# Deep attention stage: the weighted sum of the values issued in one run of 128 passes behind the turn of k, in place of two runs of 64 around it

## The chip, the cores and the metric

The kernel runs on one core of a Trainium2 chip. Its time is the device time of one execution in microseconds (us); lower is better. The engines named below are PE (TensorE, matmuls; its weight loads are listed apart as PEld), ACT (ScalarE), DVE (VectorE), POOL (GpSimd) and SP (SyncE, which issues transfers). They run side by side, each through its own instructions in program order, and wait for each other on semaphores.

## What is computed

The reference is a transformer-like chain of twelve sublayers over an activation of 4 sequences x 512 tokens x 128 values, in float32. The change lies in the sublayer that is called "deep" here: six layers of local attention and a gated feed-forward part, and the chain calls it twice. Cut to the attention:

```python
def local_attention(q, k, v):            # 16 heads of 64, windows of 32
    ...
    bk2, bv2 = (look(bk), look(bv))      # each window sees itself and the one before
    sim = jnp.einsum('bhwie,bhwje->bhwij', bq, bk2) * QK_SCALE
    sim = jnp.where(mask, -jnp.finfo(sim.dtype).max, sim)
    attn = jax.nn.softmax(sim, -1)
    out = jnp.einsum('bhwij,bhwje->bhwie', attn, bv2)
    return out.reshape(b, h, n, d)

def attn_layer(x, Wqkv, qs, ksc, Wo):
    q, k, v = jnp.split(x @ Wqkv, 3, -1)
    q = l2norm(q) * qs                   # and k alike, then both are rotated (rope)
    ...
    out = local_attention(q, k, v)
    return out.transpose(0, 2, 1, 3).reshape(b, n, INNER) @ Wo
```

## The kernel before

A call of the deep sublayer (`deep_pe` and its sisters for the other engines) works through 24 units, a unit being one of the six layers for one of the four sequences. Each unit has four tiles of 128 tokens. One loop over steps `s` from 0 to 103 is written out by hand for every engine, and it is software-pipelined: at step `s` the products of q and k are made for tile `s`, the rotated q and k of tile `s - 1` are turned (transposed), the scores and values of tile `s - 2` are made, and the weighted sum of the values of tile `s - 3` is taken. `t = s % 4` is the place of the step in its unit. What belongs to a unit and not to a tile (output projection, layer norm, feed-forward) is put between these by `t`: the variance and its spread at `t == 0`, three gate products and two of the three "a" products at `t == 1`, the last "a" product, the down projection and the first part of the output projection at `t == 2`, the rest of that projection and the mean at `t == 3`.

On PE a step is, in this order: product of q (L1321), half of the scores with the mask (L1276, L1290), values (L1346), the other half of the scores (L1290), something of the unit, **turn of q** (`turn_pe(..., 0)`, L1334, eight passes of 128x128), **product of k** (L1321, four passes of 512 columns), **first run of the weighted sum** (`mix_open_pe`, L1373, 64 passes), something of the unit at `t == 1`, **turn of k** (`turn_pe(..., 1)`, L1334, eight passes), the mean at `t == 3`, **second run of the weighted sum** (`mix_close_pe`, L1373, 64 passes), work of the unit at `t` 1 and 2, and the turn of the probabilities (L1304). A matmul of float32 shows as two passes in the trace, so 32 matmuls are 64 passes.

The turns of q, of k and of the probabilities and the values share one stretch of PSUM, `turns`. ACT copies each out before the next may be written. For the turn of k this stands in `turn_pe`, and the copy is the line below it on ACT (L1507):

```python
pe.wait_ge(de.deep_roped, 2 * i + half + 1)
if half == 1:
    pe.wait_ge(de.deep_turn_kept, 2 * i + 1)
...
nc.scalar.activation(dst, turns.rearrange("p (c t) -> p c t", t=P), ACT.Copy).then_inc(de.deep_turn_kept, 1)
```

ACT takes its work in a written order too. In a step it copies the turned probabilities (L1518), squares the product of q (L1494), takes a square root (L1501), copies the values (L1534), takes the exponential of the scores (L1511), **copies the turned q** (L1507), squares the product of k (L1494), takes the gelus at `t == 1` (L1550), copies the turned k (L1507) and copies the result of the weighted sum (L1525). The exponential waits for DVE, which takes the maximum of the scores (L1589) and subtracts it (L1596) once the second half of the scores is done. POOL scales the rotated q and k (L1753), which the turns wait for, and divides the probabilities (L1759), which their turn waits for.

Of the kernel before, what the change touches and what calls it, by code (L numbers as in the profile page):

```python
# [21 lines left out]
TILES = T // P  # L22
# [6 lines left out]
PAIRS = LHEADS // 2  # L29
# [16 lines left out]
def program(nc, d, out, sublayers):  # L46
    with ExitStack() as ctx:
# [6 lines left out]
        def bank(i):  # L54
            return psum[:, i * 512:(i + 1) * 512]
# [61 lines left out]
        def apart(eng):  # L117

            eng.sem_inc(g.waits_passed, 1)
# [1102 lines left out]
        ALL = UNITS * TILES  # L1222
# [124 lines left out]
                                            xs[unit_ % 2][:, WIN * wi:WIN * wi + 2 * WIN], vw[:, r, :, :], start=True, stop=True)  # L1347
            last.then_inc(de.deep_v_ready, 1)

        def mix_open_pe(pe, c, j):  # L1350
            i, t = c * ALL + j, j % TILES
            pe.wait_ge(de.deep_probs_kept, i + 1)
            pe.wait_ge(de.deep_v_kept, i + 1)
            pe.wait_ge(deep_v_moved[t], 16 * MOVES * (c * UNITS + j // TILES + 1))
            if j + 1 < ALL:
                pe.wait_ge(de.deep_less_max, i + 2)
            apart(pe)
            mix_pe(j, 0)

        def mix_close_pe(pe, c, j):  # L1360
            mix_pe(j, 1).then_inc(de.deep_pv_done, 1)

        def mix_pe(j, part):

            t = j % TILES
            for pair in range(PAIRS // 2 * part, PAIRS // 2 * (part + 1), 2):
                for jj in range(WPT):
                    for odd in range(2):
                        for r in range(2):
                            side = r ^ odd  # L1370
                            half, col = (pair + odd) // 4, (pair + odd) % 4 * P + jj * WIN
                            to = (pair // 2) * P + jj * WIN
                            last = nc.tensor.matmul(bank(odd)[64 * side:64 * side + 64, to:to + WIN],  # L1373
                                                    V[64 * r:64 * r + 64, WPT * t + jj, (pair + odd) * 64:(pair + odd) * 64 + 64],
                                                    probsT[64 * r:64 * r + 64, half, col:col + WIN], start=True, stop=True)
            return last

        WO_FIRST = 3

# [61 lines left out]
        def deep_pe(pe, c):  # L1441
            for s in range(LAST + 1):
                n, t = s // TILES, s % TILES
# [16 lines left out]
                    turn_pe(pe, c, s - 1, 0)  # L1460
                if s < ALL:
                    qk_pe(pe, c, s, 1)
                if 0 <= s - 3 < ALL:
                    mix_open_pe(pe, c, s - 3)
                if t == 1 and ending:
                    gate_pe(pe, c, n - 2, 1)
                if 0 <= s - 1 < ALL:
# [1 line left out]
                if t == 3 and begun:  # L1469
                    mean_pe(pe, c, n - 1)  # L1470
                if 0 <= s - 3 < ALL:
                    mix_close_pe(pe, c, s - 3)
                if t == 1 and ending:
                    gate_pe(pe, c, n - 2, 2)
                    a_pe(pe, c, n - 2, 0)
# [636 lines left out]
```

## Time and profile before

| | us |
|---|---|
| median of three runs | 4470.68 |
| lowest and highest of them | 4459.03, 4475.77 |
| the profiled execution, its own time | 4482.51 |
| its span in the trace | 4480.8 |
| PE busy in the span | 4247.5 (95%) |
| DVE busy | 3201.0 (71%) |
| ACT busy | 2674.7 (60%) |
| POOL busy | 2127.7 (47%) |

The two calls of the deep sublayer take about 1070 to 2680 us and 2840 to 4460 us of the span, 72% of it. The times of rows are microseconds from the start of the span. A busy PE is not PE at its peak: matmuls are pipelined, and the end that a row gives a run lies behind the start of the next one. So the length of a run is read from its start to the start of what follows.

### The profile page before, as it was taken

What the parts mean: (1) busy time and instruction counts of PE and PEld (TensorE: products, weight loads), DVE (VectorE), ACT (ScalarE), POOL (GpSimd) and SP (SyncE); (2) the same over time, 40 slices, a digit from 0 to 9 for tenths busy, and PEclk for the clock granted to TensorE, in tenths of its full rate; (3) what the DMA queues carried; (4) which work ended last, traced back from release to release, by engine and by line L of the source; (5) the groups of instructions that cost most, each with busy time, mean ns of one, the idle gap of its engine ahead of it and who ended that gap; (6) DMA issues with size and microseconds to landing.
All of it is one profiled execution on the core that took longest, in us unless ns stands there. A gap on an engine that the chain in (4) does not pass through costs nothing.

```text
span 4480.8 us, 148099 instructions
## 1 busy us (share of the span) xinstructions
PE 4247.5 (95%) x66444; PEld 2382.4 (53%) x66444; DVE 3201.0 (71%) x4171; ACT 2674.7 (60%) x3161; POOL 2127.7 (47%) x1151
## 2 busy tenths in 40 slices
PE   7998999867999999999999995799999999999998
PEld 4543433334555555555555552455555555555554
DVE  3564666465777777777777766687787787787784
ACT  1451355323776776776776761576776776776774
POOL 0110000013666666666666640666665665666662
PEclk8898899978999999999999997899999999999998
DMA  2000000001111112111111111111211212121111
GB/s 85 1 2 1 1 1 1 1 0 40 33 29 53 39 28 59 33 53 34 33 53 34 33 28 50 24 33 32 56 33 31 56 33 55 32 58 29 33 33 29
DMA packets 78739, 144.92 MB, mean 32 GB/s; under 512 B 18656, under 2 KB 25120, under 8 KB 76576
## 3 DMA queue, kind: packets, MB, share of 16 engines
q1 hardware_dynamic: 78112, 135.45, 11.7%
q8 instruction: 529, 8.67, 0.8%
q14 instruction: 98, 0.80, 0.1%
HBM read 39.97 MB, written 1.05 MB: 9 GB/s over the span
## 4 chain that ended last, share of the span: by engine, by line
PE 80%; POOL 7%; issue 6%; DVE 5%; ACT 2%; DMA 0%; SPq 0%; POOLq 0%; DVEq 0%; ACTq 0%
PE psum L1321 13%; PE psum L1373 7%; PE psum L1346 7%; PE psum L1334 6%; PE psum L1290 5%; PE psum L681 5%; PE psum L1392 5%; PE psum L1304 4%; PE psum L1422 3%; PE psum L713 3%; PE psum L1438 3%; PE psum L1432 3%; PE psum L735 3%; PE psum L1387 3%; POOL arena L1753 3%
## 5 line engine op out<-in xcount | busy, mean ns | idle before, releaser
L1753 POOL TENSOR_TENSOR arena<-arena 128x1024 f32<-128x1024 f32 x384 | 722.3, 1902 | 883.8 <-ACT arena L1501 883.8
L1747 POOL TENSOR_TENSOR arena<-arena 128x1024 f32<-128x1024 f32 x384 | 907.3, 2363 | 246.3 <-DVE arena L1622 246.3
L1618 DVE TENSOR_TENSOR arena<-psum,arena 128x1024 f32<-128x1024 f32 x384 | 467.6, 1218 | 619.5 <-ACT arena L1494 619.0
L1494 ACT ACTIVATE arena<-psum 128x1024 f32<-128x1024 f32 x384 | 392.0, 1021 | 288.9 <-PE psum L1321 288.9
L1373 PEld LDWEIGHTS psum<-arena 64*64 64x64 f32 x24576 | 396.4, 135 | 211.5 <-issue 211.4
L1507 ACT ACTIVATE arena<-psum 128x1024 f32<-128x1024 f32 x384 | 390.5, 1017 | 194.5 <-PE psum L1334 194.5
L1622 DVE TENSOR_TENSOR arena<-psum,arena 128x1024 f32<-128x1024 f32 x384 | 466.2, 1214 | 0.0
L1629 DVE TENSOR_REDUCE h_pair<-arena 128x16 f32<-128x1024 f32 x384 | 464.1, 1209 | 0.0
L1373 PE MATMUL psum<-arena 64*64 64x32 f32 x24576 | 438.8, 221 | 4.9 <-DVE arena L1596 4.7
L1334 PE MATMUL psum<-w_ident,arena 128*128 128x128 f32 x3072 | 416.4, 279 | 23.0 <-POOL arena L1753 14.7
L1334 PEld LDWEIGHTS psum<-w_ident,arena 128*128 128x128 f32 x3072 | 338.8, 141 | 161.0 <-POOL arena L1753 91.5
L1321 PE MATMUL psum<-deep_wqkv,arena 128*128 128x512 f32 x768 | 382.5, 622 | 26.5 <-DVE arena L1622 19.1
L1759 POOL TENSOR_TENSOR arena<-arena 128x1024 f32<-128x1024 f32 x192 | 365.3, 1902 | 69.8 <-DVE arena L1606 61.0
L1290 PEld LDWEIGHTS psum<-arena 64*32 64x32 f32 x24576 | 293.6, 105 | 169.6 <-issue 159.5
L1321 PE MATMUL psum<-arena 128*128 128x512 f32 x768 | 361.9, 592 | 0.0
L1518 ACT ACTIVATE arena<-psum 128x1024 f32<-128x1024 f32 x192 | 196.5, 1023 | 259.1 <-PE psum L1304 253.2
L1290 PE MATMUL psum<-arena 64*32 64x64 f32 x24576 | 328.2, 223 | 1.5 <-issue 1.4
L681 PE MATMUL psum<-arena 32*128 32x512 f32 (+3 forms) x1024 | 307.5, 600 | 3.3 <-ACT arena L820 2.3
L1511 ACT ACTIVATE arena<-arena 128x1024 f32<-128x1024 f32 x192 | 202.9, 1057 | 175.5 <-DVE arena L1596 175.5
L713 PE MATMUL psum<-arena 32*128 32x512 f32 (+3 forms) x1024 | 303.6, 583 | 1.8 <-ACT arena L845 1.8
L1589 DVE TENSOR_REDUCE arena<-psum 128x16 f32<-128x1024 f32 x192 | 235.1, 1225 | 63.6 <-PE psum L1290 63.6
L845 ACT ACTIVATE arena<-psum 128x512 f32<-128x512 f32 (+3 forms) x344 | 160.9, 515 | 178.6 <-PE psum L713 177.2
(266 smaller groups left out, 6997.6 us busy)
## 6 DMA issues: line engine op xcount, KB each, us to landing
arena<-arena SPq DMA_DIRECT2D x672, 128.0 KB, 2.4
deep_wqkv<-in_deep_wqkv SPq DMA_DIRECT2D x6, 1536.0 KB, 6.9
arena<-in_deep_wqkv SPq DMA_DIRECT2D x6, 1536.0 KB, 6.7
arena<-arena SPq DMA_DIRECT2D x96, 64.0 KB, 2.0
deep_wo<-in_deep_wo SPq DMA_DIRECT2D x6, 512.0 KB, 7.4
arena<-in_deep_wo SPq DMA_DIRECT2D x6, 512.0 KB, 7.4
deep_w<-in_deep_w SPq DMA_DIRECT2D x6, 341.0 KB, 7.6
arena<-in_deep_w SPq DMA_DIRECT2D x6, 341.0 KB, 7.5
```

The source lines that it names most:

```text
L681: nc.tensor.matmul(bank(v % SCORE_BANKS)[:, 0:keys], da_Q[r32, b * SETS + s, x_ * P:(x_ + 1) * P], keys_of(causal, b, s)[r32, 0:keys], sta ...
L713: nc.tensor.matmul(bank(key_at[m])[:, q0:T], kk[r32, kt * P:(kt + 1) * P], da_Q[r32, b * SETS + s, q0:T], start=True, stop=True).then_inc( ...
L1290: last = nc.tensor.matmul(bank(r)[32 * jj:32 * jj + 32, pair * 64:pair * 64 + 64], qT[j % 2][r64, pair, jj * WIN:(jj + 1) * WIN], kT[r64, ...
L1321: last = nc.tensor.matmul(bank(2 + cc), xs[unit_ % 2][:, WIN + t * P:WIN + (t + 1) * P], wqkv[:, half * INNER + cc * 512:half * INNER + (c ...
L1334: last = nc.tensor.matmul(turns[:, m * P:(m + 1) * P], roped[a % 2][:, h:h + 2, :], w.ident[:, :], start=True, stop=True, is_transpose=True)
L1373: last = nc.tensor.matmul(bank(odd)[64 * side:64 * side + 64, to:to + WIN], V[64 * r:64 * r + 64, WPT * t + jj, (pair + odd) * 64:(pair + ...
L1494: nc.scalar.activation(qk_sq[:, HALVES[half], :], qk_half, ACT.Square).then_inc(de.deep_qk_squared, 1)
L1618: nc.vector.tensor_tensor(turned[:, hs, :].rearrange("p h (a e) -> p h a e", a=2), swapped, sin, ALU.mult).then_inc(de.deep_rope_parts, 1)
L1622: nc.vector.tensor_tensor(roped[a % 2][:, hs, :], qk_half, under(tabs[:, 2 * half, t, :], shape), ALU.mult).then_inc(de.deep_rope_parts, 1)
L1629: nc.vector.tensor_reduce(h_pair[:, hs, 0], qk_sq[:, hs, :], AX.X, ALU.add).then_inc(de.deep_sq_summed, 1)
L1747: nc.gpsimd.tensor_tensor(roped[a % 2][:, hs, :], roped[a % 2][:, hs, :], turned[:, hs, :], ALU.add).then_inc(de.deep_summed, 1)
L1753: nc.gpsimd.tensor_tensor(roped[a % 2][:, hs, :], roped[a % 2][:, hs, :], over(h_inv[a % 2][:, hs], [P, LHEADS, LD]), ALU.mult).then_inc(d ...
```

## The change

The two runs of 32 matmuls become one of 64, with the same operands and targets, and it stands where the second run stood. The waits of the first run (for the turned probabilities, the values, their moves and the less-maximum of the next tile) stand ahead of the whole run now. Nothing else is moved, and no other engine's instructions change.

```diff
-        def mix_open_pe(pe, c, j):
+        def mix_pe(pe, c, j):
             i, t = c * ALL + j, j % TILES
             pe.wait_ge(de.deep_probs_kept, i + 1)
             pe.wait_ge(de.deep_v_kept, i + 1)
...
             apart(pe)
-            mix_pe(j, 0)
-
-        def mix_close_pe(pe, c, j):
-            mix_pe(j, 1).then_inc(de.deep_pv_done, 1)
-
-        def mix_pe(j, part):
-
-            t = j % TILES
-            for pair in range(PAIRS // 2 * part, PAIRS // 2 * (part + 1), 2):
+            for pair in range(0, PAIRS, 2):
...
-            return last
+            last.then_inc(de.deep_pv_done, 1)
...
                 if s < ALL:
                     qk_pe(pe, c, s, 1)
-                if 0 <= s - 3 < ALL:
-                    mix_open_pe(pe, c, s - 3)
                 if t == 1 and ending:
                     gate_pe(pe, c, n - 2, 1)
                 if 0 <= s - 1 < ALL:
...
                 if t == 3 and begun:
                     mean_pe(pe, c, n - 1)
                 if 0 <= s - 3 < ALL:
-                    mix_close_pe(pe, c, s - 3)
+                    mix_pe(pe, c, s - 3)
```

On PE, in a step with `t == 2`, the order before was this, from the turn of q to the down projection (a row is a group of equal instructions, with the semaphores that its first one waits for; `arena` holds most tiles):

```order
L1334 MATMUL psum<-w_ident,arena 128x128 [waits deep_v_kept,deep_roped]
L1334 MATMUL psum<-w_ident,arena 128x128 x7
L1321 MATMUL psum<-deep_wqkv,arena 128x512 [waits deep_rope_parts]
L1321 MATMUL psum<-deep_wqkv,arena 128x512
L1373 MATMUL psum<-arena 64x32 [waits deep_less_max,deep_v_moved_3,deep_probs_kept,deep_v_kept]
L1373 MATMUL psum<-arena 64x32 x31
L1334 MATMUL psum<-w_ident,arena 128x128 [waits deep_turn_kept,deep_roped]
L1334 MATMUL psum<-w_ident,arena 128x128 x7
L1373 MATMUL psum<-arena 64x32 x32
L1438 MATMUL psum<-arena,deep_w_0 128x512 [waits deep_hidden_ready]
```

The same place of the changed kernel, where the weighted sum has line 1365 and the down projection line 1430:

```order
L1334 MATMUL psum<-w_ident,arena 128x128 [waits deep_v_kept,deep_roped]
L1334 MATMUL psum<-w_ident,arena 128x128 x7
L1321 MATMUL psum<-deep_wqkv,arena 128x512 [waits deep_rope_parts]
L1321 MATMUL psum<-deep_wqkv,arena 128x512
L1334 MATMUL psum<-w_ident,arena 128x128 [waits deep_turn_kept,deep_roped]
L1334 MATMUL psum<-w_ident,arena 128x128 x7
L1365 MATMUL psum<-arena 64x32 [waits deep_less_max,deep_v_moved_3,deep_probs_kept,deep_v_kept]
L1365 MATMUL psum<-arena 64x32 x63
L1430 MATMUL psum<-arena,deep_w_0 128x512 [waits deep_hidden_ready]
```

The turn of k, which waits for `deep_turn_kept`, now follows the product of k at once; 32 matmuls that stood between them have gone behind it.

## Rows read from the trace of the kernel before

**Rows 1.** Busy time by engine in an early step and in most of a call.

```profile
core 0: us, PE busy (x) PEld busy (x) DVE busy (x) ACT busy (x) POOL busy (x), PEclk, DMA share, GB/s
1120.81:1134.46 13.65, 12.43 (x306) 7.95 (x305) 11.45 (x13) 10.79 (x11) 10.34 (x6) 1.00 0.13 31
1150.00:2640.00 1490.00, 1483.08 (x27972) 876.59 (x27973) 1163.10 (x1325) 1047.87 (x1107) 948.13 (x484) 1.00 0.16 39
```

**Rows 2.** What line 1334, the turns of q and k, waited for: us, times.

```profile
  POOL arena L1753: 106.3, 111
...
  ACT arena L1507: 4.4, 4
```

**Rows 3.** Timeline of PE and ACT, a step with t == 2: start, us.

```profile
2151.91 1.88 PE L1321 MATMUL psum<-deep_wqkv,arena 128*128 128x512 f32 x4
...
2152.49 1.06 ACT L1511 ACTIVATE arena<-arena 128x1024 f32<-128x1024 f32 x1 [0.97 <-DVE arena L1596]
2153.46 1.00 ACT L1507 ACTIVATE arena<-psum 128x1024 f32<-128x1024 f32 x1
...
2153.72 1.14 PE L1373 MATMUL psum<-arena 64*64 64x32 f32 x64
...
2154.79 1.09 PE L1334 MATMUL psum<-w_ident,arena 128*128 128x128 f32 x8
...
2156.88 2.85 PE L1438 MATMUL psum<-arena 128*128 128x512 f32 x6
```

**Rows 4.** Timeline, step 96 of the first call, which has no product of k.

```profile
2658.93 1.00 ACT L1507 ACTIVATE arena<-psum 128x1024 f32<-128x1024 f32 x1
...
2660.08 1.06 PE L1334 MATMUL psum<-w_ident,arena 128*128 128x128 f32 x8 [0.75 <-ACT arena L1507]
...
2661.08 0.78 PE L1373 MATMUL psum<-arena 64*64 64x32 f32 x39
...
2662.05 0.59 PE L1373 MATMUL psum<-arena 64*64 64x32 f32 x25 [0.20 <-issue]
```

**Rows 5.** Timeline of PE, step 98 of the second call, with no turn of k.

```profile
4439.38 2.07 PE L1373 MATMUL psum<-arena 64*64 64x32 f32 x128
4441.37 2.84 PE L1438 MATMUL psum<-arena 128*128 128x512 f32 x6
4444.06 2.74 PE L1387 MATMUL psum<-arena 128*128 128x512 f32 x6
4446.63 4.46 PE L1392 MATMUL psum<-arena 128*128 128x512 f32 x10
```

**Rows 6.** Timeline of PE and ACT, a step with t == 0, and ACT behind it.

```profile
2120.81 1.88 PE L1321 MATMUL psum<-deep_wqkv,arena 128*128 128x512 f32 x4
...
2122.37 1.00 ACT L1507 ACTIVATE arena<-psum 128x1024 f32<-128x1024 f32 x1
...
2126.04 1.09 PE L1304 MATMUL psum<-w_ident,arena 128*128 128x128 f32 x8 [0.19 <-POOL arena L1759]
...
2127.50 1.88 PE L1321 MATMUL psum<-deep_wqkv,arena 128*128 128x512 f32 x4
...
2129.42 1.02 ACT L1494 ACTIVATE arena<-psum 128x1024 f32<-128x1024 f32 x1 [1.23 <-PE psum L1321]
```

**Rows 7.** Timeline of PE and ACT, the step behind it, t == 1.

```profile
2135.01 1.88 PE L1321 MATMUL psum<-deep_wqkv,arena 128*128 128x512 f32 x4
...
2136.58 1.01 ACT L1507 ACTIVATE arena<-psum 128x1024 f32<-128x1024 f32 x1
...
2140.88 1.09 PE L1422 MATMUL psum<-xc,arena 128*85 128x512 f32 x2
```

**Rows 8.** Timeline of PE and ACT, a step with t == 3.

```profile
2105.66 1.04 PE L1334 MATMUL psum<-w_ident,arena 128*128 128x128 f32 x8
...
2106.53 1.89 PE L1321 MATMUL psum<-arena 128*128 128x512 f32 x4
2106.73 1.02 ACT L1507 ACTIVATE arena<-psum 128x1024 f32<-128x1024 f32 x1 [1.79 <-PE psum L1334]
...
2112.36 1.09 PE L1304 MATMUL psum<-w_ident,arena 128*128 128x128 f32 x8
```

## Prediction

> **What bounds the kernel now.** I read the table of busy times by stretch first, to see which engine has no slack in the stage that changes. Over 1490 us of the first call PE is busy for 1483.08, at a granted clock of 1.00, while DVE, ACT and POOL rest for a fifth or more of it [rows 1]. So the stage is as long as PE's passes and waits. A change that only reorders PE can do two things: alter what it costs to go from one kind of pass to another, or let PE run into a wait that other passes had covered.
>
> Next I read the timelines of PE and ACT, one step of each kind, and ask for each wait that the change touches: when does it end, and when does PE get there? The turn of k writes where the turn of q stands, so it waits until ACT has copied q out. In the step with `t == 2` that copy runs from 2153.46 to 2154.46, because it is queued behind the exponential, which itself waited for DVE [rows 3]. PE finishes the product of k and begins the weighted sum at 2153.72. The first run of the sum lasts until 2154.79, so it covers the end of the copy with 0.33 to spare. The list of what line 1334 waited for agrees: ACT's copy held it only 4 times [rows 2]. The change takes this cover away.
>
> **The prices.** All from start to start.
> - After a copy's end the turn of k starts 0.15 later: the copy of [rows 4] ends at 2659.93 and the turn starts at 2660.08. That row is the wait itself, seen in the one step that lacks the product of k.
> - A turn that has waited takes 1.00 to the next run (2660.08 to 2661.08) [rows 4]. An unhindered one takes 0.87 (2105.66 to 2106.53) [rows 8], or 0.109 a pass.
> - A weighted sum in one run of 128 passes takes 1.99, from 4439.38 to 4441.37 [rows 5]. That is the changed kernel's run already. One run of 64 takes 1.07 (2153.72 to 2154.79) [rows 3], two of them 2.14, so joining saves 0.15.
> - A 512-column pass takes 0.43: six take 2.57 (4444.06 to 4446.63) [rows 5]. Four before a sum take 1.81 (2151.91 to 2153.72) [rows 3] where 4 x 0.43 is 1.71, so going over to the small passes costs 0.10.
>
> At this place the Trainium skill has a rule that speaks for the change. Its page TensorEngine Tiling (Key Properties) says that a change of tiling mode drains TensorE. The trace agrees that a switch costs something; by that rule alone the change would gain some 45 us, which is the first rival below, worked out there from rows.
>
> **The change, step by step.** I count from the start of the product of k and ask when the work behind the sum begins.
>
> *t == 2.* The copy ends at 2.55 (2154.46 less 2151.91). Then 0.15, the turn 1.00, the sum 1.99: 5.69. Before it was 4.97 (2156.88 less 2151.91) [rows 3]. Loss **0.72**. PE stands idle from 1.71 to 2.70, some 1.0 us.
>
> *t == 0.* The copy ends at 2.56, so the sum ends at 5.70. Before, the turn of the probabilities began at 5.23, having waited 0.19 for POOL's division [rows 6]; that wait vanishes, and the loss is 0.47. Behind it twelve short passes took 1.46 until 2127.50, more than 12 x 0.109 plus some 0.06 for leaving the small passes, 1.37. I let 0.09 of it be waiting that is now covered. Loss **0.38**.
>
> *t == 1.* Here a gate product of two passes, 0.86, moves in between: PE is there at 1.71 + 0.86 = 2.57. The copy ends at 2.58 (2137.59 less 2135.01), the turn starts at 2.73, the sum ends at 5.72. Before: 5.87 (2140.88 less 2135.01) [rows 7]. Gain **0.15**.
>
> *t == 3.* Much work lies between the scores and the turn of q, so the copy is done at 1.22 (2107.75 less 2106.53) and nothing waits. 1.71 + 0.87 + the mean 0.86 + 0.10 + 1.99 = 5.53, against 5.83 (2112.36 less 2106.53) [rows 8]. Gain **0.30**.
>
> What is queued behind the waiting turn on PE is the sum, and for the sum wait ACT's copy of its result and the turn of the probabilities. Both lie on PE's own path here, so they are late by what PE is late. The waits that the sum itself had now end earlier against it, and cost nothing. The copy of the turned k has more time before its next user than before.
>
> Counts for one call, from the loop: 23 steps with `t == 2`, 22 with `t == 0`, 22 with `t == 1`, 23 with `t == 3`, and the three first steps with a sum, which have no unit's work yet and lose like `t == 0` without the spread, 0.47. That is 23 x 0.72 = 16.6, plus 22 x 0.38 = 8.4, plus 3 x 0.47 = 1.4, less 22 x 0.15 = 3.3, less 23 x 0.30 = 6.9: 16.2 us. The last steps of a call, where the sum waits for something else and a gate product can now fill that wait, may give 1 back. Two calls: 2 x 15.2, **30 us**. Against the profiled execution's 4482.5 that is 4513; against the median of the runs, 12 lower, 4501.
>
> Bounds. If the waiting turn takes 0.93 in place of 1.00 and starts 0.12 behind the copy, the 140 steps that wait lose 0.10 less each, 14 us. If the joined run saves nothing (2.14 in place of 1.99), 186 steps lose 0.15 more, 28 us. So the forecast's own range is +16 to +58.
>
> **The rivals.**
>
> *Faster: the copy does not hold the turn.* Then each step keeps only the saved switches: at `t == 2` 4.97 less (1.71 + 0.87 + 0.10 + 1.99 = 4.67) is 0.30, at `t == 1` 0.34, at `t == 3` 0.30, at `t == 0` nothing, since POOL's division still ends at 5.23. About 0.94 a unit, 48 units: 45 us less, 4426. It decides itself where the copy ends before 1.71 less 0.15, at 1.56; it ends at 2.55 or more in three steps of four [rows 3, 6, 7], and no moved instruction makes ACT or DVE earlier. Chance 0.07.
>
> *No change: the loss is given back.* The turn of q waits for POOL, 106.3 us in 111 waits [rows 2]. If the steps now come late enough for POOL to be ready, a quarter of that, some 25 us, returns: +5, 4476. Against it: the chain to POOL begins with ACT's square, and ACT sat idle for 1.23 before that until PE's product was there [rows 6]. A late PE makes POOL late by as much. Chance 0.13.
>
> *Slower still.* In [rows 4] a run of the sum breaks for 0.20 with nothing to wait for but its instructions. If a burst of 128 passes brought that in each of 186 steps, 37 us come on top: 4538. The unbroken run of [rows 5] is against it. The other form is the clock. Were it granted at 1.2 GHz in place of 2.4, the 12.43 busy us of a step would cost as much again; one step in ten would be 230 us. The early step has PE idle for 1.22 of 13.65 us at a granted clock of 1.00 [rows 1], which is the idleness that I expect. Chance 0.10, of which the clock 0.02.
>
> The Trainium skill's page TensorE: Matmul & The Clock Gate (Why this matters for your kernels) warns of idle gaps between bursts for the clock's sake. The early step's row speaks for gaps of this size being harmless.
>
> *The change does nothing:* something that I have not seen bounds the step. Chance 0.02.
>
> **How the numbers follow.** The forecast has 0.68, and I predict its time, 4501. The bound of half a per cent, which is about what a measurement of this kernel can tell from no change, is 22 us; the forecast's 30 lies close above it, so I give 0.60 of its chance to slower and 0.08 to no change. Slower: 0.60 + 0.10 and 0.01 for what I have not seen, 0.71. The same: 0.08 + 0.13 + 0.01, 0.22. Faster: 0.07. The range holds the forecast and the case of a loss given back: 4474 to 4530.
>
> **What the changed profile would show.** Line 1334 waiting for ACT L1507 some 140 times, about 1.0 us each at `t` 0 and 2, 0.2 or less at `t == 1` and never at `t == 3`. The sum in runs of 128 passes of 1.99. No wait for POOL L1759 ahead of the turn of the probabilities. Steps of `t` 1 and 3 shorter. I am wrong if the copy of q ends earlier against the product of k than 2.55, if PE's granted clock drops inside the stage, or if the runs of the sum are broken.

## The result, and the profile after

| | before | changed |
|---|---|---|
| median of four runs, us | 4465.39 | 4537.76 |
| lowest and highest, us | 4459.03, 4475.77 | 4524.98, 4545.29 |
| ratio, with its 95% interval | | 1.0160 (1.0132 to 1.0188) |
| span of the profiled execution, us | 4480.8 | 4543.5 |
| PE busy in the span, us | 4247.5 | 4216.9 |

The change costs 72 us, 1.6%. The direction was forecast, the size was not: 4501 was predicted, and 4538 lies outside the range.

The busy times by stretch show at once what kind of loss it is. Both rows run from the first to the last mask passes of the first call, 95 steps, in the kernel before and in the changed one (the columns are those of [rows 1]):

```profile
1081.40:2664.10 1582.70, 1565.45 (x29827) 929.30 (x29826) 1234.41 (x1401) 1113.53 (x1174) 1012.89 (x516) 1.00 0.16 39
```

```profile
1090.30:2702.90 1612.60, 1549.33 (x29827) 925.29 (x29826) 1233.49 (x1401) 1109.33 (x1174) 1012.53 (x516) 1.00 0.16 39
```

The same 29827 passes at the same granted clock. PE is busy for 16.1 us less, so the joined runs do save switches, and the stretch is 29.9 us longer, so PE rests for 46 us more. Two kinds of rest are to be found.

**The first is the wait that was forecast.** What line 1334, the turns, waited for in the changed kernel (the same view as [rows 2]; ACT's copy is line 1497 now, and POOL's multiply L1743):

```profile
  POOL arena L1743: 105.9, 110
  ACT arena L1497: 87.6, 105
```

The waits for POOL are as they were, the waits for ACT are new. This view counts the gaps of the weight loads beside those of the matmuls. Of the matmuls alone, POOL held 14.7 us in 11 waits before and 15.3 in 11 after, and ACT 4.4 in 4 before and the same 87.6 in 105 after. So 91.6 of POOL's 106.3 us in [rows 2] were gaps between weight loads, under which PE's matmuls went on.

This is the timeline of PE and ACT in one step with `t == 2`, which answers to [rows 3]:

```profile
2113.84 1.89 PE L1321 MATMUL psum<-arena 128*128 128x512 f32 x4
2114.44 1.06 ACT L1501 ACTIVATE arena<-arena 128x1024 f32<-128x1024 f32 x1 [0.97 <-DVE arena L1586]
2115.40 1.00 ACT L1497 ACTIVATE arena<-psum 128x1024 f32<-128x1024 f32 x1
...
2116.55 1.07 PE L1334 MATMUL psum<-w_ident,arena 128*128 128x128 f32 x8 [0.83 <-ACT arena L1497]
2117.55 2.07 PE L1365 MATMUL psum<-arena 64*64 64x32 f32 x128
...
2119.55 1.98 PE L1430 MATMUL psum<-arena 128*128 128x512 f32 x4
```

Read it downward: the copy of the turned q ends at 2116.40, the turn of k starts 0.15 later, the sum 1.00 behind that, and it lasts 2.00. From the product of k to the work behind the sum it is 5.71.

**The second is not in any wait on an engine.** A step with `t == 0` in the second call, which waits for ACT's copy in the same way (timeline of PE alone, changed kernel):

```profile
4064.48 1.07 PE L1334 MATMUL psum<-w_ident,arena 128*128 128x128 f32 x8 [0.81 <-ACT arena L1497]
4065.47 1.95 PE L1365 MATMUL psum<-arena 64*64 64x32 f32 x118
4070.84 0.64 PE L1365 MATMUL psum<-arena 64*64 64x32 f32 x10 [3.43 <-issue]
4071.41 1.97 PE L1304 MATMUL psum<-w_ident,arena 128*128 128x128 f32 x8
```

The sum stops after 118 of its 128 passes, and the last ten follow more than three microseconds later. "issue" means that PE waited for nothing that the profile shows. What the matmuls of line 1365, the sum, waited for over the span:

```profile
  issue: 15.6, 18
  DVE arena L1586: 1.7, 2
```

The length of a step, from its mask passes (L1276) to those of the next, keeps the two apart. Below are the medians over some 22 steps of each kind in both calls, then the time from the first to the last such start of each call, then how much steps 8 to 94 are above their medians in sum, and the breaks (from one pass to the next over 0.13 us) inside runs of 64-row passes, of the sum and of the scores, with their sum.

| kernel, profiled execution | t=0 | t=1 | t=2 | t=3 | call 1 | call 2 | above the medians | breaks in the sum, in the scores |
|---|---|---|---|---|---|---|---|---|
| before | 14.21 | 16.91 | 18.61 | 17.52 | 1582.7 | 1586.0 | 0.1 + 1.2 | 2, 4 (3.0 us) |
| changed | 14.59 | 16.74 | 19.35 | 17.24 | 1612.6 | 1621.5 | 13.1 + 19.3 | 20, 7 (24.8 us) |

The medians changed by +0.38, -0.17, +0.74 and -0.28, where the prediction had +0.38, -0.15, +0.72 and -0.30. With its counts that is 16.6 a call, some 32 for both less what their ends give back. The two calls are 65.4 longer. The other half is irregular: of 174 steps, 144 are within 0.15 us of their median or below it, and 30 are 0.2 to 6.2 us above it.

### Where the runs break

I numbered PE's instructions in the trace, weight loads, passes and semaphore instructions together: 135,549. All 27 breaks of the changed kernel and all 6 of the kernel before, that of [rows 4] among them, fall at a number that leaves 193 or 194 when divided by 256. So do all 228 breaks in the kernels of the experiments below. The queues of the changed kernel have this row:

```profile
q8 instruction: 529, 8.67, 0.8%
```

135,549 / 256 is 529.5, so one packet of this queue, 16.4 KB, carries 256 of PE's instructions. I call these 256 a block, and the place between two blocks a border. A sum in one run is 128 weight loads and 128 passes, 256 instructions in 2.0 us. Between the first and the last mask passes of a call, the shortest time that any 256 successive instructions take is 1.84 us in the changed kernel; before it was 2.89.

Packets and borders can be counted against each other. In both kernels a break ends 2.2 to 2.9 us after the start of one certain packet, and its number is always the border's own less one, so this is the packet that brings the instructions behind the border. In none of the traces here does PE pass a border inside a call sooner than 2.15 us after the start of its packet. So the theory that the runs below test: **the instructions behind a border can be used some 2.2 us or more after their packet starts, and PE stands when it is there sooner.** The expectations below were written with a simpler form of it, that PE waits when it has used up a block in much less than 3 us. How long the block itself has lasted is not the measure, though. The packet that ends a break starts 0.3 to 4.3 us after PE passed the border before, and the sum also broke in blocks that PE had begun more than 5 us earlier.

What counts is that nearly the whole block can lie behind the packet's start. In 19 of the changed kernel's 20 breaks of the sum PE was 251 to 141 instructions short of the border when the packet started, and in a joined run it is through these in 2 us or less. The 20 joined runs of the changed kernel broke at instruction 227 to 253 of their 256: only a border near the end of a run breaks it. Four steps are 2555 instructions, 5 less than ten blocks, so the border wanders by 5 from unit to unit, and the break comes and goes.

The largest breaks stand in steps in which SP loads a layer's weights. The busy times around the one above, PE first, then after the granted clock the share of the DMA engines:

```profile
4060.00:4065.00 5.00, 4.12 (x25) 2.76 (x25) 4.89 (x6) 4.11 (x5) 4.99 (x3) 1.00 0.62 144
4065.00:4070.00 5.00, 2.42 (x123) 2.14 (x121) 4.05 (x5) 1.27 (x2) 4.96 (x3) 0.92 0.97 393
4070.00:4075.00 5.00, 4.16 (x24) 3.58 (x25) 0.69 (x1) 2.05 (x2) 0.23 (x1) 0.50 0.37 130
```

The DMA engines are full, and the packet of instructions starts only when PE has come to the last instruction ahead of the border. Behind the long rest PE's clock is granted at 0.50, its lower level of 1.2 GHz, so that these few microseconds cost again. Between steps 8 and 94 of the calls it fell at one other place, behind a break of 1.47 us that followed a wait of 0.81 for ACT:

```profile
3997.00:4002.00 5.00, 4.87 (x29) 3.64 (x28) 1.50 (x4) 2.05 (x2) 1.74 (x1) 0.66 0.01 3
```

The gaps of 0.8 in every other step leave it at 1.00 where no break follows: so it is in padclean below, which has the same gaps and no break.

### The profile page after: what moved, and what is told of

It reads as the page before. It is cut to its first block, busy times and chain, and to the rows that moved or that the text cites. A ratio compares the mean times of both kernels' runs of the same rounds, so it can differ in the third digit from the quotient of the medians.

```text
span 4543.5 us, 148099 instructions
## 1 busy us (share of the span) xinstructions
PE 4216.9 (93%) x66444; PEld 2377.9 (52%) x66444; DVE 3199.8 (70%) x4171; ACT 2665.1 (59%) x3161; POOL 2127.1 (47%) x1151
## 4 chain that ended last, share of the span: by engine, by line
PE 79%; DVE 8%; issue 8%; ACT 3%; POOL 0%; DMA 0%; SPq 0%; POOLq 0%; DVEq 0%
PE psum L1321 11%; PE psum L1365 8%; PE psum L1346 8%; PE psum L1290 6%; PE psum L1334 6%; PE psum L681 5%; PE psum L1384 5%; PE psum L1304 4%; DVE arena L1579 3%; DVE arena L1586 3%; PE psum L713 3%; PE psum L1430 3%; PE psum L735 3%; PE psum L1414 3%; PE psum L1379 3%
## 5 line engine op out<-in xcount | busy, mean ns | idle before, releaser
L1743 POOL TENSOR_TENSOR arena<-arena 128x1024 f32<-128x1024 f32 x384 | 722.2, 1902 | 940.9 <-ACT arena L1491 940.9
L1484 ACT ACTIVATE arena<-psum 128x1024 f32<-128x1024 f32 x384 | 392.3, 1022 | 280.7 <-PE psum L1321 280.7
L1334 PE MATMUL psum<-w_ident,arena 128*128 128x128 f32 x3072 | 412.5, 278 | 106.7 <-ACT arena L1497 87.6
L1497 ACT ACTIVATE arena<-psum 128x1024 f32<-128x1024 f32 x384 | 390.2, 1016 | 126.2 <-PE psum L1334 126.2
L1365 PEld LDWEIGHTS psum<-arena 64*64 64x64 f32 x24576 | 381.7, 135 | 81.5 <-issue 81.3
L1365 PE MATMUL psum<-arena 64*64 64x32 f32 x24576 | 404.9, 220 | 17.4 <-issue 15.6
L1321 PE MATMUL psum<-deep_wqkv,arena 128*128 128x512 f32 x768 | 377.7, 616 | 26.3 <-DVE arena L1612 19.3
L1508 ACT ACTIVATE arena<-psum 128x1024 f32<-128x1024 f32 x192 | 196.5, 1023 | 251.3 <-PE psum L1304 245.9
L1515 ACT ACTIVATE arena<-psum 128x1024 f32<-128x1024 f32 x192 | 196.6, 1024 | 204.2 <-PE psum L1365 204.2
```

What stands on the lines that cost most here:

```text
L1321: last = nc.tensor.matmul(bank(2 + cc), xs[unit_ % 2][:, WIN + t * P:WIN + (t + 1) * P], wqkv[:, half * INNER + cc * 512:half * INNER + (c ...
L1334: last = nc.tensor.matmul(turns[:, m * P:(m + 1) * P], roped[a % 2][:, h:h + 2, :], w.ident[:, :], start=True, stop=True, is_transpose=True)
L1484: nc.scalar.activation(qk_sq[:, HALVES[half], :], qk_half, ACT.Square).then_inc(de.deep_qk_squared, 1)
L1743: nc.gpsimd.tensor_tensor(roped[a % 2][:, hs, :], roped[a % 2][:, hs, :], over(h_inv[a % 2][:, hs], [P, LHEADS, LD]), ALU.mult).then_inc(d ...
```

## The experiments

All runs in one table. Ratios are against the kernel before, timed on the same chip; n is the number of runs of the kernel.

| kernel | median us (n) | ratio (95%) | t=0 | t=1 | t=2 | t=3 | call 1 | call 2 | breaks in the sum, all breaks |
|---|---|---|---|---|---|---|---|---|---|
| copyfirst | 4518.99 (4) | 1.0117 (1.0079 to 1.0155) | 14.59 | 17.59 | 18.34 | 17.24 | 1610.5 | 1620.1 | 14, 19.7 us |
| joined13 | 4459.53 (10) | 0.9989 (0.9967 to 1.0011) | 14.21 | 16.74 | 18.61 | 17.24 | 1580.3 | 1576.2 | 11, 11.9 us |
| padsafe | 4524.70 (4) | 1.0132 (1.0096 to 1.0169) | 14.59 | 16.73 | 19.35 | 17.24 | 1608.9 | 1617.1 | 7, 11.2 us |
| padworst | 4618.41 (4) | 1.0340 (1.0303 to 1.0378) | 14.59 | 17.16 | 19.59 | 17.24 | 1659.1 | 1640.4 | 86, 85.7 us |
| joined123 | 4459.03 (11) | 0.9966 (0.9945 to 0.9988) | 14.21 | 16.74 | 18.33 | 17.24 | 1580.6 | 1579.4 | 20, 17.1 us |
| sumfirst | 4500.36 (1) | one run | 14.97 | 16.61 | 18.29 | 17.77 | 1600.4 | 1604.5 | 9, 12.2 us |
| split123 | 4651.60 (1) | one run | 14.58 | 17.83 | 20.89 | 17.56 | 1670.8 | 1684.6 | 6, 14.4 us |
| beforepad | 4483.77 (1) | one run | 14.21 | 16.91 | 18.61 | 17.52 | 1584.9 | 1581.8 | 2, 7.0 us |
| padclean | 4518.55 (6) | 1.0124 (1.0100 to 1.0149) | 14.58 | 16.73 | 19.35 | 17.23 | 1601.1 | 1603.2 | none |
| mixed | 4439.76 (12) | 0.9943 (0.9924 to 0.9962) | 14.21 | 16.61 | 18.29 | 17.23 | 1574.6 | 1568.0 | 15, 16.7 us |
| mixedclean | 4447.91 (12) | 0.9973 (0.9954 to 0.9993) | 14.21 | 16.61 | 18.29 | 17.24 | 1563.9 | 1567.4 | 0, 0.2 us |
| padspread | 4516.61 (6) | 1.0133 (1.0104 to 1.0162) | 14.58 | 16.73 | 19.35 | 17.23 | 1618.1 | 1600.6 | 1, 1.6 us |
| mixedspread | 4452.57 (12) | 0.9983 (0.9962 to 1.0004) | 14.21 | 16.61 | 18.29 | 17.24 | 1582.7 | 1567.9 | 2, 3.8 us |

### The wait: copyfirst, and joined13

copyfirst is the changed kernel with the exponential behind the copy of the turned q at `t` 1 and 2, so that the copy no longer queues behind it:

```diff
                     value_act(act, c, s - 2)
-                    exp_act(act, c, s - 2)
+                    if t not in (1, 2):
+                        exp_act(act, c, s - 2)
                 if 0 <= s - 1 < ALL:
                     turn_act(act, c, s - 1, 0)
+                if 0 <= s - 2 < ALL and t in (1, 2):
+                    exp_act(act, c, s - 2)
```

> The changed kernel, and on ACT, at t 1 and 2, the copy of the turned q ahead of the exponential instead of behind it. Theory (the turn of k is held by that copy): the copy then ends about 1.2 us after the start of the product of k in place of 2.55, line 1334 no longer waits for it at t 1 and 2, steps of t == 2 take 18.3 us in place of 19.35 and those of t == 1 16.55 in place of 16.74; t 0 and 3 stay. That is 45 to 60 us less than the changed kernel, less what breaks of PE's instruction supply add or take (up to 20 us either way): 4470 to 4500 against a kernel before at 4468. Rival (the wait for the copy is a symptom and something else bounds the step): the time stays within 15 us of the changed kernel, 4523 or more.

What line 1334 waited for in copyfirst, beside 87.6 us in 105 waits in the changed kernel:

```profile
  ACT arena L1497: 44.3, 50
```

At `t == 2` the wait is gone and the step takes 18.34, as expected: the queue on ACT is what held the turn. The whole time missed its expectation, 4519 and not 4470 to 4500, because at `t == 1` the step grew, to 17.59. Such a step in the changed kernel, and then in copyfirst:

```profile
2163.86 1.28 ACT L1501 ACT_TABLE_LOAD   x1
2165.25 1.88 PE L1321 MATMUL psum<-deep_wqkv,arena 128*128 128x512 f32 x4
2165.86 1.06 ACT L1501 ACTIVATE arena<-arena 128x1024 f32<-128x1024 f32 x1 [0.72 <-DVE arena L1586]
...
2170.06 1.26 ACT L1540 ACTIVATE arena<-psum,arena 128x512 f32<-128x512 f32 x2
```

```profile
2154.15 1.88 PE L1321 MATMUL psum<-deep_wqkv,arena 128*128 128x512 f32 x4
2154.35 1.02 ACT L1497 ACTIVATE arena<-psum 128x1024 f32<-128x1024 f32 x1 [1.61 <-PE psum L1334]
2155.39 1.28 ACT L1501 ACT_TABLE_LOAD   x1
2156.69 1.06 ACT L1501 ACTIVATE arena<-arena 128x1024 f32<-128x1024 f32 x1
...
2158.68 1.28 ACT L1540 ACT_TABLE_LOAD   x1
2159.97 1.26 ACT L1540 ACTIVATE arena<-psum,arena 128x512 f32<-128x512 f32 x2
2160.71 0.23 PEld L1414 LDWEIGHTS psum<-xc,arena 128*85 128x85 f32 x2 [1.06 <-ACT arena L1540]
```

The load of the exponential's table used to run while ACT waited for DVE. Behind the copy it stands in the path, 1.28 between the copy and the exponential. Counted from the product of k, the gelus start at 5.82 (2159.97 less 2154.15) in place of 4.81, and PE's gate product waits for those. Moving an activation moved its table load too.

joined13 is the kernel before with the sum in one run behind the turn of k only where no wait was forecast, at `t` 1 and 3:

```diff
-                if 0 <= s - 3 < ALL:
+                if 0 <= s - 3 < ALL and t not in (1, 3):
                     mix_open_pe(pe, c, s - 3)
...
                 if 0 <= s - 3 < ALL:
+                    if t in (1, 3):
+                        mix_open_pe(pe, c, s - 3)
                     mix_close_pe(pe, c, s - 3)
```

> The kernel before, with the weighted sum in one run behind the turn of k at t 1 and 3 only; at t 0 and 2 it keeps its two runs. Theory: the steps of t 1 and 3 gain 0.17 and 0.28 each, t 0 and 2 are as before: 20 us less, and 10 to 20 us more from breaks in the joined runs at t == 1, so between -12 and 0 us against the kernel before, and no wait of line 1334 for ACT above 0.2. Rival (any joined run costs, wherever it stands): 15 us or more above the kernel before.

Both kinds of step are as short as in the changed kernel, and the other two as before. That is 0.45 a unit. The two calls are 12 us shorter in the profiled execution, and the timed runs cannot tell the kernel from the one before (the interval holds 1). So the losses at `t` 0 and 2 are the change's, one by one, and the gains at 1 and 3 can be had alone, less what 11 breaks in the sum take.

### The blocks: padsafe and padworst

Both are the changed kernel with five semaphore increments more on PE in a unit, which make it 2560 instructions, ten blocks. The borders then stand still against the steps. padworst puts 90 and 84 more ahead of the two calls, which move them to where they fall near the ends of the sums. Nothing is waited for anew.

```diff
+        def spare(pe, n):
+
+            for _ in range(n):
+                apart(pe)
+
         def deep_pe(pe, c):
...
                 n, t = s // TILES, s % TILES
+                if t == 0 and s < ALL:
+                    spare(pe, 5)
...
                 elif kind == "deep":
+                    spare(pe, (90, 84)[call])
                     quad_stats_pe(pe, u, q)
```

(padsafe has the first two pieces only.)

> The changed kernel with 240 empty semaphore increments on PE, five ahead of each unit, so that a unit has 2560 of PE's instructions, ten times 256. Theory (PE's instructions arrive in blocks of 256, and PE waits when one block is used up in much less than 3 us, as in the last tenth of a run of the sum of 256 instructions): with these the borders of the blocks never fall into instructions 226 to 256 of a run, so no run of the sum breaks; the steps take 14.59, 16.74, 19.35 and 17.24 us by t, without outliers but for the loads of a layer, and the kernel takes 25 to 40 us less than the changed one, 4498 to 4512, some 30 above the kernel before. Rival (breaks come from the length of the run or from other transfers, whatever the borders): as many breaks as in the changed kernel, within 10 us of its time.

> The same five empty increments ahead of each unit, and 90 and 84 more ahead of the first and second call, so that the borders fall into the last tenth of a run in every unit: at t 0 and 2 in the first call, at t 1 and 3 in the second. Theory: a break of 0.4 to 1.5 us in nearly 90 runs, 75 us above the other padded kernel (50 to 100), 4560 to 4600. Rival (the borders don't matter): the same time as the other padded kernel within 10 us.

The work is the same, PE has the same passes in the same order, and the one kernel is 94 us slower than the other (4618.41 less 4524.70). padworst has 86 breaks in the sum, where nearly 90 were expected. What the sum's matmuls waited for in it, where it was 15.6 us in 18 waits in the changed kernel, and one such step:

```profile
  issue: 62.1, 78
```

```profile
2113.23 1.06 PE L1334 MATMUL psum<-w_ident,arena 128*128 128x128 f32 x8 [0.83 <-ACT arena L1504]
2114.22 1.93 PE L1365 MATMUL psum<-arena 64*64 64x32 f32 x115
2116.73 0.42 PE L1365 MATMUL psum<-arena 64*64 64x32 f32 x13 [0.58 <-issue]
```

That the place of the border decides is hard to read in another way. 74 of the 94 us are in the two calls (3299.5 against 3226.0); the increments themselves take some of the rest, as the last runs show. padsafe missed its expectation. The small breaks are gone, but eight steps that load weights are 1.6 to 4.6 us longer each, and the steps are still 20.5 us above their medians, where the changed kernel has 32.4. In the second call these breaks fall outside the runs that the table counts. This is one of them, at the same remainder, 193:

```profile
3237.86 0.45 PE L1403 MATMUL psum<-w_ident,rstd 128*128 128x128 f32 x2 [2.59 <-issue]
```

A border that is safe with idle DMA engines is not safe with full ones.

### The length of the run: sumfirst and split123

sumfirst joins the sum ahead of the turn of k, directly behind the product of k, so that four passes of 512 columns stand before it. split123 parts the sum of the changed kernel at `t` 1 to 3 again, with other work between the halves, and leaves it whole at `t == 0`.

```diff
                     qk_pe(pe, c, s, 1)
+                if 0 <= s - 3 < ALL:
+                    mix_pe(pe, c, s - 3)
...
-                if 0 <= s - 3 < ALL:
-                    mix_pe(pe, c, s - 3)
```

```diff
                     gate_pe(pe, c, n - 2, 2)
+                if t == 1 and 0 <= s - 3 < ALL:
+                    mix_rest_pe(pe, c, s - 3)
...
                     down_pe(pe, c, n - 2)
+                if t == 2 and 0 <= s - 3 < ALL:
+                    mix_rest_pe(pe, c, s - 3)
...
                     probs_turn_pe(pe, c, s - 2)
+                if t == 3 and 0 <= s - 3 < ALL:
+                    mix_rest_pe(pe, c, s - 3)
```

> One look. The changed kernel with its one run of the sum where the first run stood, ahead of the turn of k. Theory: the run of 1.99 covers ACT's copy, so line 1334 never waits for it, but the turn of the probabilities now meets the copy of the turned k at t 0 and 3: steps of some 14.9, 16.7, 18.4 and 17.7 us by t. Ahead of the run stands the product of k with 8 instructions in 1.7 us in place of the turn's 16 in 1.0, so 256 instructions that end late in a run last 3.2 us and more in place of 1.9 to 2.8: at most 6 breaks in the sum against 20 in the changed kernel, all for borders behind instruction 248 of the run. Rival (the length of the run makes the breaks, wherever it stands): 15 or more breaks in the sum.

> One look. The changed kernel with both halves of the sum still behind the turn of k, but at t 1, 2 and 3 parted by what stood next (a gate product, the down projection, the turn of the probabilities); t 0 keeps its run of 128 passes. Theory: the turn waits for ACT's copy as in the changed kernel, each parting costs about 0.15, so steps of 14.59, 16.9, 19.5 and 17.4; no break in the sum at t 1 to 3, and breaks only where a border falls in the last tenth of a run at t 0. Rival (breaks come from the wait ahead of the sum): breaks at t 2 as often as before.

sumfirst had 9 breaks in the sum, more than the 6 that I allowed and fewer than the rival's 15. This run settles nothing on what the passes ahead of a run do. It shows something else. Ahead of the turn of k the joined sum is a gain at `t` 1 and 2 (16.61, 18.29) and a loss at 0 and 3 (14.97, 17.77). split123 had its 6 breaks in the sum all at `t == 0`, where the run was left whole, and none in the runs of 64 of the other steps. Both are single executions. In them the length of the run decides, though runs of 64 passes break now and then in other kernels, two in the kernel before. Its time missed widely. The halves that come late hold up the copy of the sum's result, and with it the gate and output products at `t` 1 and 2, which I had not costed.

### A control, and no break at all: beforepad and padclean

beforepad is the kernel before with the five increments a unit. padclean is the changed kernel with them and with the borders moved to where they fall neither into the last tenth of a sum nor into the early part of a step that loads weights:

```diff
             for i, (kind, b) in enumerate(TM_ORDER):
+                if (kind, b) == ("o", 0):
+                    spare(pe, 213)
...
                     forget_in_pe(pe, u, q)
+                    spare(pe, 116)
```

> One look. The kernel before with the 240 empty increments of the first padded kernel. It is the control for them: steps of 14.21, 16.91, 18.61 and 17.52 us by t as without them, and a total within the spread of the kernel before, 4448 to 4481, breaks at most at the loads of a layer. Rival (the increments themselves cost time): steps of t == 0 longer by 0.1 or more.

> The changed kernel with empty increments on PE, five ahead of each unit and 116 and 213 more in places where PE waits for other engines anyway (in the forget and the time sublayers), so that the borders of the blocks of 256 instructions fall neither into the last tenth of a run of the sum nor into the first two thirds of the step in which a layer's weights are loaded. Theory: no break above 0.6 at all; steps of 14.59, 16.74, 19.35 and 17.24 us by t, so the two calls of the deep stage take 30 to 33 us more than in the kernel before, and the kernel 25 to 38 us more, ratio 1.0055 to 1.0085. That is the part of the change's cost that is the wait for the copy; the first padded kernel's breaks were all at the loads. Rival (other breaks come in their place): within 10 us of the changed kernel, ratio 1.013 or more.

beforepad's two calls take 3166.7, against 3168.7 before: five increments a unit cost nothing that can be seen in this single execution. padclean has not one break. The step that broke for 3.43 in the changed kernel, in padclean, with the DMA share of its stretch (the sum is line 1367 here):

```profile
4046.96 1.06 PE L1336 MATMUL psum<-w_ident,arena 128*128 128x128 f32 x8 [0.81 <-ACT arena L1506]
4047.96 2.07 PE L1367 MATMUL psum<-arena 64*64 64x32 f32 x128
4049.96 1.09 PE L1306 MATMUL psum<-w_ident,arena 128*128 128x128 f32 x8
```

```profile
4047.00:4052.00 5.00, 5.00 (x150) 4.50 (x151) 4.57 (x8) 3.67 (x4) 4.94 (x4) 1.00 0.99 349
```

The same wait on ACT, the same full DMA engines, and no break. So the load of the weights alone is harmless here; it is the load together with a border at a bad place that costs microseconds. The two calls take 3204.3: 29.8 less than the changed kernel's 3234.1, which is the price of the blocks, and 35.6 more than before's 3168.7, which is the price of the wait, and what the prediction put at 30. The whole time missed its expectation, 1.24% and not 0.55 to 0.85. The profile finds the rest where the 213 increments stand, between the calls: 185.2 there in place of some 168. The product behind them shows it:

```profile
2785.27 3.75 PE L1153 MATMUL psum<-arena,w_tm_wo 128*128 128x512 f32 x4 [27.66 <-issue]
```

In the trace these increments follow each other every 0.15 us, 32 us for 213. In the changed kernel PE waited 12.55 us for DVE at this place, which hides a part of them.

### Joined where it pays: joined123, mixed, mixedclean

joined123 is the kernel before with the sum joined behind the turn at `t` 1 to 3, and the copy ahead of the exponential at `t == 2`. mixed takes the better place of each kind of step: ahead of the turn at 1 and 2, behind it at 3, two runs at 0. mixedclean is mixed with padclean's increments.

```diff
                 if 0 <= s - 3 < ALL:
-                    mix_open_pe(pe, c, s - 3)
+                    if t != 3:
+                        mix_open_pe(pe, c, s - 3)
+                    if t in (1, 2):
+                        mix_close_pe(pe, c, s - 3)
...
-                if 0 <= s - 3 < ALL:
+                if 0 <= s - 3 < ALL and t in (0, 3):
+                    if t == 3:
+                        mix_open_pe(pe, c, s - 3)
                     mix_close_pe(pe, c, s - 3)
```

> The sum in one run behind the turn of k at t 1, 2 and 3; at t 0 the two runs of the kernel before; and at t == 2 alone ACT copies the turned q ahead of the exponential. Theory (the copy's hold and the borders of blocks of 256 instructions are all that the change costs): steps of 14.21, 16.74, 18.34 and 17.24 us by t, against 14.21, 16.91, 18.61 and 17.52 before, 33 us less, and 5 to 20 us back from breaks in joined runs: 13 to 28 us below the kernel before, ratio 0.994 to 0.997. Rival (joined runs have a cost that moves to whatever step is joined): no gain over the kernel before.

> Each kind of step with its best place for the sum: at t 1 and 2 one run ahead of the turn of k, at t == 3 one run behind it, at t == 0 the two runs of the kernel before. Theory: steps of 14.21, 16.61, 18.29 and 17.24 us by t, 40 us less than before in all, and 10 to 20 us back from breaks where borders fall late in a joined run: ratio 0.993 to 0.996. Rival (such gains are eaten by new waits): 0.998 or more.

> The same with the empty increments that put the borders where nothing breaks. Theory: no break in the sum or at the loads, so the full 40 us less than the kernel before: ratio 0.989 to 0.993, and 10 to 20 us below the same kernel without them. Rival (the increments cost what they save): no more than 5 us between the two.

joined123 came out as expected, 0.34% below the kernel before (0.12 to 0.55). mixed is the fastest of all, 0.57% below it (0.38 to 0.76). The sum ahead of the turn covers ACT's copy with 2.00 in place of 1.07, and the medians give 0.30, 0.32 and 0.29 a unit, some 42 us in all, of which the breaks leave 26 in the profiled calls. PE's timeline of a step with `t == 3`, from the product of k to the turn of the probabilities 5.55:

```profile
2112.76 1.89 PE L1321 MATMUL psum<-arena 128*128 128x512 f32 x4
2114.49 1.04 PE L1334 MATMUL psum<-w_ident,arena 128*128 128x128 f32 x8
2115.36 1.02 PE L1400 MATMUL psum<-xn,w_avg 128*128 128x512 f32 x2
2116.31 2.07 PE L1373 MATMUL psum<-arena 64*64 64x32 f32 x128
2118.31 1.29 PE L1304 MATMUL psum<-w_ident,arena 128*128 128x128 f32 x8
```

mixedclean takes the breaks away but for one of 0.2, its calls are 11 us shorter still, and it is no faster in the whole: between the calls it takes 184.3 in place of 166.3. The increments cost what they save, and the 0.989 to 0.993 that was expected did not come.

### What an increment costs: padspread and mixedspread

In these two the 213 increments between the calls are replaced by 13 in each of the last steps of the first call, and 5 in one more, where I hoped that PE's waits would hide them:

```diff
+                if c == 0 and ALL - 16 <= s <= ALL:
+                    spare(pe, 13 if s < ALL else 5)
```

> The changed kernel with increments in the same places. Theory (the change's cost is 33 us of waiting for the copy and some 33 of breaks): without breaks but for up to 8 us in those sixteen steps it takes 30 to 40 us more than the kernel before, ratio 1.007 to 1.0095, half of what the changed kernel shows. Rival (the lower sum of the steps is not seen in the whole time): ratio 1.012 or more.

> The kernel of the best places with the same borders, but the 213 increments for the second call no longer stand in the time sublayer, where they cost 17 us (184 us between the calls' steps in place of 167); thirteen stand ahead of each of the last sixteen steps with a product of the first call, and five behind. Theory: PE reads them ahead of its passes there and they cost next to nothing; the borders roam in those sixteen steps alone, for some 5 us of breaks at most. Steps as in that kernel, 165 to 170 us between the calls, 34 to 40 us less than the kernel before: ratio 0.990 to 0.994. Rival (an increment costs its 0.08 us wherever it stands): 184 us are saved there and come back inside the call, ratio 0.995 or more.

The rival won in the whole times. Of the steps from 79 on, in which the 13 stand, those of `t == 2` are no longer than without them, and the others are 0.4 to 2.8 us longer, 17.5 in sum in mixedspread and 15.0 in padspread. So 213 increments cost some 17 us at both places, 0.08 each in the mean. That is a balance and no price of one: they take 0.15 each where they follow each other, and what PE would have waited anyway hides the rest. Five at the start of a unit are not seen. The second call of padspread has none of the 213, and one break of 0.4: 1600.6, against 1586.0 before and 1621.5 changed. So of the 35.5 that this call lost, some 15 are the wait and some 21 the breaks.

## Why the prediction was right and wrong

**Right: what bounds the stage, and the wait.** The product of k to the work behind the sum was forecast as 5.69, 5.70, 5.72 and 5.53 at `t` 2, 0, 1 and 3. The changed kernel's timelines have 5.71 (2113.84 to 2119.55), 5.70, 5.71 and 5.54, each step of the way with its own term: copy, 0.15, turn 1.00, sum 2.00. The sum of the terms was 30 for two calls, padclean has 35.6. The bounds taken from rows held: the turn that waited took 1.00, the joined run saved 0.15. One count was off without a consequence: the profile names ACT for 105 waits where I had some 140, since at `t == 1` the turn starts 0.15 behind the copy without an entry.

**Right: no gain, and no loss given back.** The waits on POOL's multiply stayed, 106.3 us before [rows 2] and 105.9 after, and the steps kept their whole loss at the medians. A late PE made POOL late by as much, as the prediction argued. The rival "the loss is given back" was weaker than its text has it, though: it took the 106.3 for time in which PE stood, and the matmuls' own part of it was 14.7, so there were never 25 us to come back.

**Wrong: "That is the changed kernel's run already".** The step that failed is the price of the joined run, 1.99 from [rows 5], taken for every step. The run is 2.00 when it is whole, but it is also as many instructions as a block has, and 20 runs in the changed kernel's profile broke. The row was one execution of the run at one place against the blocks. One unbroken sample was evidence of how long a whole run takes, and none on how often it is whole. Two of the signs that the prediction named for being wrong came: the runs of the sum were broken, and the granted clock dropped inside the stage. The missing term measured 29.8 us in the two calls (changed less padclean), about as much as all terms that were there. The two calls are 65.4 longer in the profiled executions, whose spans differ by 62.7, and the medians differ by 72.4. That difference is not explained, and lies within the spread: executions of one kernel are 17 to 20 us apart here.

**The rival that had it.** "Slower still" named the break of [rows 4], "with nothing to wait for but its instructions", and gave 4538. The measured time is 4537.76, but the agreement is partly luck: the rival had 0.20 in each of 186 steps, and it is 27 breaks of 0.14 to 3.65 us, of which the largest stands in a step that is 6.2 longer. I gave it 0.10 because "the unbroken run of [rows 5] is against it". Had I listed all six breaks of the kernel before and not the one, their common remainder by 256 was there to be seen, and with it that a run of 256 instructions in 2 us uses them up faster than anything that the calls had in their steps, 2.89 us. The range ended at 4530 because this rival was priced as unlikely and left out of it.

**The clock** was the smaller form of that rival, and it took part: not by the gaps of 0.8 us alone, which leave it at 1.00, but behind two breaks, of 3.65 and of 1.47 us. The Trainium skill's page TensorE: Matmul & The Clock Gate (Why this matters for your kernels) warns of long idle gaps between bursts. The granted clock agrees in that it fell behind the longest rest and not behind those of 0.8. It also fell behind the break at 3997, and not behind others of the same length, such as the one of 1.57 at 3890.

**Still open.** Why a packet starts 0.3 us behind the border before in one place and 4.3 in another was not tried, nor whether other passes ahead of a run can make it safe.

## What to carry to other kernels

Before two runs are joined or a wait is moved, ask what the piece between them was covering: the first run covered the end of ACT's copy, and the place of each step kind has to be chosen by that, not one place for all. Count the instructions of the densest stretch as well as its time: many small passes with a weight load each can use up their instructions faster than they are fetched, and the loss then shows as "issue" inside a run, in a few steps only, and moves when anything ahead of it adds an instruction. So compare medians of steps and the sum above them apart, and list every break before calling a run unbroken.

## What the runs showed of the hardware that was not expected

- PE's instructions come in packets of 256 (16.4 KB, 529 packets for 135,549), and no border was passed sooner than 2.15 us after the start of its packet. In a run of 256 instructions in 2.0 us PE stood for 0.1 to 1.6 us when the border fell at instruction 227 or later, and for 3.65 when a load of weights filled the DMA engines. The runs of 64 passes, 128 instructions in 1.07 us, broke twice in the kernel before and never in the one execution of split123.
- The place of a program against these blocks is worth 74 us in the two calls here with the same passes (padworst 3299.5, padsafe 3226.0), as much as the change under study.
- Semaphore increments on PE follow each other every 0.15 us. 213 of them made the kernel some 17 us longer, as PE would have waited for a part of their 32 us anyway, and five in a unit of 67 us cost nothing that can be seen (beforepad).
- After a rest of 3.43 us the granted clock was 0.50 for the next stretch of 5 us, and 0.66 in the 5 us around the end of a rest of 1.25 that came 3 us behind one of 0.81. Rests of 0.8 us alone, two in a unit of 68 us, left it at 1.00 (padclean).
